# Second expert stage: the square of relu on VectorE, from the gate bank and the relu tile

## The reference, cut to what matters

```python
W1e = w1.reshape(D, E, W).transpose(1, 0, 2)      # E = 8 experts, W = 128
W2e = w2.reshape(E, W, D)
h = jnp.einsum('td,edw->etw', xf, W1e)
a = jnp.square(jax.nn.relu(h))
y = jnp.einsum('etw,ewd->etd', a, W2e)
out = jnp.einsum('etd,te->td', y, cw)             # cw: weights of the two best experts, else 0
```

```python
q = jax.nn.elu(q) + 1.0
k = jax.nn.elu(k) + 1.0
kv_state = jnp.einsum('bhnd,bhne->bhde', k, v)
attn_out = jnp.einsum('bhnd,bhde->bhne', q, kv_state)
denom = jnp.maximum(jnp.einsum('bhnd,bhd->bhn', q, k_state), 1e-06)[..., None]
attn_out = (attn_out / denom).transpose(0, 2, 1, 3).reshape(b, s, d)
```

## Time and profile before

| what | value |
|---|---|
| three runs of the kernel | 1939.63, 1934.07, 1939.16 us (median 1939.16) |
| the profiled execution | 1942.1 us, its span 1940.4 us |
| the second expert stage in the profile | about 1108 to 1350 us, 64 chunks |
| mean granted TensorE clock over the span | 0.92 of full |
| relu of chunk 0 starts | 1108.88 us |
| relu of chunk 63 starts | 1337.93 us |

### The profile page before, as it was taken

How to read it: one execution, slowest core, us unless ns; L and a number is a source line. 1 busy time by engine, 2 the same in 40 slices (tenths; PEclk the granted TensorE clock), 3 DMA queues, 4 the chain that set the end, 5 groups by cost and what they waited for, 6 DMA issues and landing times.

```text
span 1940.4 us, 25449 instructions
## 1 busy us (share of the span) xinstructions
PE 1724.4 (89%) x8004; PEld 1318.3 (68%) x8004; DVE 1185.5 (61%) x2758; ACT 979.3 (50%) x1906; POOL 852.3 (44%) x866
## 2 busy tenths in 40 slices
PE   6989998779999899999999888889899888888799
PEld 6979997757767677776767655656665555555565
DVE  5542215767677777767686825444356666677765
ACT  3612001656556656565656667666545444445442
POOL 3841201335555545454545453444457666651100
PEclk9989558789999999999999989898899888889999
DMA  6001001087332323233223452221001101002233
GB/s 85 1 2 24 1 1 33 17 198 180 107 93 91 98 85 98 88 98 93 93 88 118 122 149 66 66 86 42 28 12 33 29 23 23 23 31 74 81 109 93
DMA packets 131183, 134.92 MB, mean 70 GB/s; under 512 B 56614, under 2 KB 75306, under 8 KB 131050
## 3 DMA queue, kind: packets, MB, share of 16 engines
q1 hardware_dynamic: 120904, 132.35, 24.5%
q10 hardware_dynamic: 10146, 0.94, 0.6%
HBM read 127.93 MB, written 5.31 MB: 69 GB/s over the span
## 4 chain that ended last, share of the span: by engine, by line
PE 39%; DVE 18%; ACT 12%; issue 7%; POOL 4%; DMA 2%; SPq 1%; DVEq 0%; ACTq 0%; POOLq 0%
PE ypsum L1156 7%; PE flow_G L100 4%; PE flow_G L102 3%; PE flow_G L101 3%; DVE flow_a L1701 2%; DVE flow_a L1707 2%; PE flow_U L100 2%; DVE flow_phi L1485 2%; PE flow_U L101 2%; PE flow_U L102 2%; POOL flow_alo L1790 2%; ACT flow_ahi L1186 1%; ACT xn_tokens L1218 1%; PE flow_side L100 1%; DVE flow_at_rneg L1673 1%
## 5 line engine op out<-in xcount | busy, mean ns | idle before, releaser
L1790 POOL TENSOR_TENSOR flow_alo<-flow_a,flow_ahi 128x512 fp32r<-128x512 f32 x264 | 341.6, 1294 | 339.8 <-ACT flow_ahi L1186 339.3
L100 PE MATMUL flow_G<-xn_hi,flow_hi 128*128 128x512 f32 x520 | 283.9, 546 | 37.6 <-DVE flow_a L1701 22.4
L1701 DVE TENSOR_TENSOR flow_a<-flow_G,flow_mask 128x512 f32<-128x512 f32 x256 | 175.7, 686 | 160.8 <-ACT flow_G L1360 135.4
L1360 ACT ACTIVATE flow_G<-flow_G 128x512 f32<-128x512 f32 x256 | 149.0, 582 | 141.1 <-PE flow_G L102 140.5
L101 PE MATMUL flow_G<-xn_lo,flow_hi 128*128 128x512 f32 x520 | 212.6, 409 | 0.0
L102 PE MATMUL flow_G<-xn_hi,flow_lo 128*128 128x512 f32 x520 | 212.1, 408 | 0.0
L1707 DVE TENSOR_TENSOR flow_a<-flow_U,flow_a 128x512 f32<-128x512 f32 x296 | 204.7, 691 | 9.9
L1186 ACT ACTIVATE flow_ahi<-flow_a 128x512 fp32r<-128x512 f32 x264 | 165.4, 627 | 86.6 <-DVE flow_a L1707 85.5
L1799 POOL TENSOR_TENSOR flow_b<-flow_b,flow_mask 128x512 f32<-128x512 f32 x96 | 126.8, 1327 | 148.5 <-ACT flow_b L1364 77.7
L1799 POOL TENSOR_TENSOR flow_a<-flow_a,flow_mask 128x512 f32<-128x512 f32 x96 | 127.8, 1342 | 105.8 <-ACT flow_a L1364 54.4
L100 PEld LDWEIGHTS flow_G<-xn_hi,flow_hi 128*128 128x128 f32 x520 | 102.2, 197 | 103.9 <-issue 42.2
(11 more groups left out here) (535 smaller groups left out, 3936.3 us busy)
## 6 DMA issues: line engine op xcount, KB each, us to landing
flow_mask<-mask_rows_top SPq DMA_DIRECT2D x512, 128.0 KB, 3.0
flow_mask<-mask_rows_top SPq DMA_DIRECT2D x64, 256.0 KB, 3.2
flow_mask<-mask_rows_zone SPq DMA_DIRECT2D x64, 256.0 KB, 3.2
flow_mask<-mask_rows_steps SPq DMA_DIRECT2D x32, 256.0 KB, 4.0
x<-in_L_attn_x SPq DMA_DIRECT2D x8, 256.0 KB, 5.9
flow_raw<-in_L_ffn_expert_gate_k SPq DMA_DIRECT2D x16, 128.0 KB, 3.6
flow_raw<-in_L_ffn_expert_up_k SPq DMA_DIRECT2D x16, 128.0 KB, 3.6
flow_raw<-in_L_ffn_expert_down_k SPq DMA_DIRECT2D x16, 128.0 KB, 3.9
```

The lines of the kernel that those rows point to most:

```text
L100: pe.matmul(out, w_hi, x_hi, start=start, stop=False)
L1360: act.activation(gate, gate, ACT.Silu).then_inc(ev["r_done"], 1)
L1701: dve.tensor_tensor(out, G[at % 2].psum[:, :], weight, ALU.mult).then_inc(ev["t_done"], 1)
L1790: pool.tensor_tensor(alo[i][:, :], acts[i][:, :], ahi[i][:, :].bitcast(F32), ALU.subtract)\
```

## The change

The square leaves ScalarE. VectorE gets an instruction per chunk of the second stage that reads the gate bank and the relu tile and writes max(gate, 0) times relu to the tile. It waits for relu of its own chunk and stands at the end of VectorE's pass for that chunk, behind that chunk's side steps. The semaphore `square` is raised by VectorE now, and the gate bank is freed by it instead of by relu. GpSimd's wait for `square` stays as it is. No transfer is added or moved.

```diff
@@ gate_up
-                    if h.direct:
+                    if h.kind == "relu2":
+                        gate.until(ev["square"], at - first + 1)
+                    elif h.direct:
                         gate.until(ev["r_done"], at + 1)
@@ scalar engine
-                def squared(at):
-                    act.wait_ge(ev["r_done"], at + 1)
-                    act.activation(b_tile(at)[:, :], b_tile(at)[:, :], ACT.Square).then_inc(ev["square"], 1)
-
@@ scalar engine, loop
                         rounded(at - 1)
-                    elif at and at - 1 < hosts[1].end:
-                        squared(at - 1)
@@ vector engine
+                def squared(at):
+                    dve.wait_ge(ev["r_done"], at + 1)
+                    dve.scalar_tensor_tensor(out=b_tile(at)[:, :], in0=G[at % 2].psum[:, :], scalar=0.0, in1=b_tile(at)[:, :],
+                                             op0=ALU.max, op1=ALU.mult).then_inc(ev["square"], 1)
+
@@ vector engine, loop
                         scale(at)
+                    elif at < plan.end and plan.chunk[at][0].kind == "relu2":
+                        squared(at)
```

## The result

The change makes the kernel slower. The median of 8 runs is 1949.78 us (1945.39 to 1951.06), against 1939.39 for 8 runs of the kernel before; the ratio is 1.0048 [1.0030, 1.0065], so about 9.3 us. I had said 1948.1, 8.9 us slower. The profiled execution took 1950.09 us, 8.0 more than the profiled one of before.

The account below looks back on a forecast made before the run. TensorE was taken as the busiest engine, 203.7 of the stage's 242 us, so its waits decide. Losses 18.0 less gains 9.1 gave 8.9 us slower: 1948.1 us as a median, range 1937 to 1957.

Parts of the forecast that it names:

- Attend behind the pile: Chunks 32 and 48: attend starts 3.9 and 3.2 us later behind VectorE's add, statistics and routing; 7.1 us lost.
- The clock at chunk 32: Attend at chunk 32: after a longer wait four pairs of matmuls run at half the clock; 1.9 us lost.
- Divide: Chunks 41 and 58: divide stands behind a square, delaying the turn that needs its bank; 1.1 and 1.3 us lost.
- Handovers at chunks 19, 29, 35 and 45: Banks handed over within one chunk: x_turn at 19 and 35, affinities at 29 and 45, start later; 5.6 us lost.
- Rows at chunks 56 and 64: TensorE's wait for ScalarE's copy of routing rows shrinks by 1.0 us at each of the two chunks.
- The same handover at chunks 23, 39, 55 and 63 falls into a longer wait: Bank handovers at these four chunks fall into a longer TensorE wait and were charged no loss.
- A removal can give back at most about this: Second expert stage: the square's 4 to 5% of the chain, roughly 10 us, caps what removing it returns.
- Gains: Relief of ScalarE's and GpSimd's queues and an earlier constants' load: 2.0 + 2.9 + 2.4 + 1.8 = 9.1 us.
- 18.0 us of losses: Attend piles 7.1, clock 1.9, divides 2.4, handovers 5.6 and two small ones 1.0, laid against TensorE's earlier starts.
- The relief wins: Rival: chunks 3 to 24 and 49 to 64, shorter ScalarE and GpSimd queues make it faster, 1931 us; 11%.
- VectorE paces the stage: Rival: VectorE, busy 154 us plus waits, falls behind relu so losses stand alone, 1957 us; 15%.
- The delays swallow each other: Rival: a third to all of the net loss goes as later waits shrink, 1937 to 1945 us; 31%.

Follow-up runs that it names:

- the ten squares back on ScalarE: Changed kernel, but ScalarE makes the squares of chunks 18, 22, 28, 34, 38, 40, 44, 54, 56 and 62 one chunk late; 1.0000 against the kernel before.
- GpSimd told in time: Square left out, relu goes into the product, GpSimd waits for relu of the same chunk; 0.9881 against the kernel before, 0.9939 when told one relu late.
- the wait alone: Kernel before, plus VectorE waiting for each chunk's relu and writing one element per partition, squares still on ScalarE; 1.0083 against the kernel before.
- the load that costs nothing: Kernel before, plus a VectorE reduction of about 0.68 us in each second-stage chunk, without waiting for relu; 1.0005 against the kernel before.
- the two sets: Changed kernel with four squares before piles and ten before handovers and divides back on ScalarE; both 0.9965, separately 1.0001 and 1.0000, against the kernel before.
- the four squares back: Changed kernel, but ScalarE makes the squares of chunks 30, 31, 46 and 47 one chunk late, as before; 1.0001 against the kernel before.

## Why the prediction was right, and where it was not

**The net was right for the reasons given, place by place, with some luck in the clock.** The forecast by chunk keeps within 2.5 us of the trace at the six chunks of the table. Attend behind the pile: 6.84 and 4.94 us of waiting, 3.7 and 2.4 more than before where I had 3.9 and 3.2. The clock at chunk 32: the pair at 1.06, as told; the busy time of chunks 24 to 31 rose by 3.6 us where I charged 1.9. Over the whole stage, though, the clock's term has the other sign: busy time fell by 1.2 us where I had 1.9 more, and idle time rose by 8.4 where I had 7.0. These two errors cancel in part, which is luck. Divide: 1.86 and 1.25 us of waiting at chunks 42 and 58, against 1.1 and 1.3. Handovers at chunks 19, 29, 35 and 45: 2.08, 1.24, 1.24, 1.24, together 5.8 against 5.6. Rows at chunks 56 and 64: 3.96 became 1.53.

**Two of the gains hit chunk 24 together, not each by itself.** The constants' copy came 26.3 us after relu of chunk 0 and not 29.2, 2.9 us sooner where I had 1.8, and by chunk 12 the stage is 3.4 us ahead. From chunk 16 to 24 it gains only 0.5 more; my terms there (2.4 and 0.5, less 1.2 for chunk 19) make 1.7.

**"The same handover at chunks 23, 39, 55 and 63 falls into a longer wait" held.** All four appear in the waits, at 1.24 us each, but each is taken out of the wait behind it. In front of chunk 56 it is 1.24 + 1.53 = 2.77 us where 3.96 less my 1.0 is 2.96, and the same at chunk 64. At chunk 24 it is 1.24 + 0.95 = 2.19 us where 2.89 less my 0.5 is 2.39. At chunk 40 it is 1.24 + 2.12 = 3.36 against 3.47; with the ten squares back on ScalarE, chunk 38's among them, x_turn at chunk 39 does not wait and attend waits 3.40.

**"A removal can give back at most about this", 10 us, failed; it is the step that was mis-sized.** I read the square's share in the chain of waits as a ceiling. Removing it is worth 23.1 us. The chain counts the time in which the square itself was the last link; it does not count what stood behind a late product (GpSimd's shift, VectorE's moments, pos_q), because there the links carry other names. The 77.7 us in the earlier trace rows that I called mostly harmless had this in it: GpSimd told in time is worth 11.3 us. Nor does it count the clock. Under "Gains" the clock's term was missing: for the same 796 instructions TensorE's busy time falls from 200.1 to 184.8 us as the granted clock rises from 0.88 to 0.95.

**"18.0 us of losses" was too low by nearly the same amount.** Against what the relief makes possible, the change gives up 23.1 + 9.3 = 32.4 us; by the wait alone it is 16 us. I had laid each loss against the start that TensorE had before, which is right for the net and blind to what the order hides. That is why the sum came out although neither side did.

**Attend at chunk 40** was forecast as 0.4 us of loss. With the wait at chunk 39 the idle time is 0.1 us less than before; what chunks 32 to 39 gave back is the clock. Before, attend was bound here by GpSimd's shift, which I had not looked at.

**The rivals.** "The relief wins" had the right engine queues and lost only by the order: with the square one chunk late it is what happens, at twice the price I gave it. "VectorE paces the stage" is refuted by the load that costs nothing, and by the same 64 squares costing nothing one chunk late. "The delays swallow each other" is not seen beyond the noise: handed back together, the two sets return 16.1 us, and one by one 9.1 + 9.3 = 18.4.

## What to carry to other kernels

Moving work to an engine with room cost nothing here by its length and much by its place: in an engine that runs its list in order, a per-chunk step that waits for this chunk's data ties every side step behind it to the chunk. Put it one chunk late, behind the side steps, when the consumer allows; here that turned 9 us slower into 18 us faster with one condition changed. Cut stages at the same work in both kernels before comparing: idle time and clock then fall apart into two numbers, and the share of an instruction in the chain of waits is no bound on what its removal gives.

## What the runs showed of the hardware

The granted clock was worth as much as the waits themselves, in these two profiles: 15.3 us of busy time against 13.0 of idle time between the kernel before and the one without squares. The Trainium skill (TensorE: Matmul & The Clock Gate, Part 1) says that idling drops the array to 1.2 GHz; the stages agree, with 0.88 at 38.3 us idle, 0.92 at 29.9 and 0.95 at 25.3, but the changed kernel has 0.90 at 46.7. So the sum of idle time does not fix the clock, nor does the length of the last wait: attend ran at the full clock (pair 0.59) after 3.18 us of idle at chunk 32 before and at half of it (pair 1.06) after 2.57 at chunk 48 before. Even the same waits give both: with the four squares back, 1.24 us at chunk 39 and 2.12 at chunk 40 stood in front of attend as in the change, and its pairs took 0.92 and then 1.06 us, where the change has 0.59. What separates these cases no run here shows.
